# Masked copies of two units by one transfer per head, and the second unit's level products behind the turned attention

## The reference, cut to what matters

```python
xn = _ln(x, ln1_w, ln1_b); sx = _token_shift(xn, state[:, i1])
xxx = jnp.tanh((xn + sx * maa_x) @ maa_w1)...           # five mixes
w = jnp.exp(-jnp.exp(time_decay + jnp.tanh(x5[:, :, 1] @ decay_w1) @ decay_w2))
r, k, v = ...  ; g = jax.nn.silu(x5[:, :, 4] @ Wg.T)
def step(s, rkvw):
    a = k_t[:, :, :, None] * v_t[:, :, None, :]
    out = jnp.einsum('bhk,bhkd->bhd', r_t, u * a + s)
    return (a + w_t[:, :, :, None] * s, out)
att = group_norm(outs) * gn_w + gn_b
x = x + att * g @ Wo.T
xn2 = _ln(x, ln2_w, ln2_b); sx2 = _token_shift(xn2, state[:, i0])
rr = jax.nn.sigmoid((xn2 + sx2 * ffn_maa_r) @ ffn_Wr.T)
kk = jnp.square(jax.nn.relu((xn2 + sx2 * ffn_maa_k) @ ffn_Wk.T))
return x + rr * (kk @ ffn_Wv.T)
```

## Time and profile before

| | before |
|---|---|
| median of three runs | 1507.39 us |
| lowest, highest | 1506.85, 1512.62 us |
| the profiled execution | 1505.76 us |
| its span | 1504.0 us |
| TensorE matmuls busy | 1438.4 us, 96% |
| VectorE, ACT, POOL busy | 60%, 34%, 40% |
| rm copies | 1024 issues of 12 KB |
| s0 loads (S0, S1) | 32 issues of 256 KB |

### The profile page before, as it was taken

How to read it: one execution, slowest core, us unless ns; L and a number is a source line. 1 busy time by engine, 2 the same in 40 slices (tenths; PEclk the granted TensorE clock), 3 DMA queues, 4 the chain that set the end, 5 groups by cost and what they waited for, 6 DMA issues and landing times.

```text
span 1504.0 us, 51989 instructions
## 1 busy us (share of the span) xinstructions
PE 1438.4 (96%) x22954; PEld 1071.4 (71%) x22954; DVE 909.6 (60%) x1990; ACT 517.6 (34%) x911; POOL 599.2 (40%) x528
## 2 busy tenths in 40 slices
PE   8998999999999999999999999999999999999898
PEld 7776876767777676876767777676876767777464
DVE  3667557664675657657574775656657564665542
ACT  1323433323333333432433333333423433332332
POOL 3353516235362433616235362433616235262421
PEclk9999999999999999999999999999999999999899
DMA  8011101011110111101011010111102011010110
GB/s 311 7 49 44 41 26 57 17 41 54 32 59 7 41 54 38 55 22 61 18 41 54 29 56 13 41 55 38 55 10 73 17 41 54 14 55 15 57 31 28
DMA packets 56448, 68.11 MB, mean 45 GB/s; under 512 B 23264, under 2 KB 40032, under 8 KB 55200
## 3 DMA queue, kind: packets, MB, share of 16 engines
q1 hardware_dynamic: 56224, 64.79, 13.9%
HBM read 43.75 MB, written 8.39 MB: 35 GB/s over the span
## 4 chain that ended last, share of the span: by engine, by line
PE 81%; DVE 9%; SPq 4%; issue 2%; DMA 2%; ACT 1%; POOL 1%; DVEq 0%; ACTq 0%; POOLq 0%
PE pairs L1227 31%; PE pairs L1246 20%; PE at_ps L1155 4%; PE pairs L1238 4%; SPq L404 3%; PE at_ps L1148 3%; DVE x L781 3%; PE pairs L1254 3%; PE pairs L1270 2%; PE att_ps L1218 2%; PE pairs L1293 2%; PE pairs L1338 1%; PE pairs L1311 1%; PE pairs L1305 1%; DVE sx L881 1%
## 5 line engine op out<-in xcount | busy, mean ns | idle before, releaser
L1227 PE MATMUL pairs<-x,wts 128*128 128x256 f32 x1760 | 397.0, 380 | 1.1 <-DVE lag L805 0.4
L1227 PEld LDWEIGHTS pairs<-x,wts 128*128 128x128 f32 x1760 | 328.4, 190 | 51.2 <-issue 7.1
L978 ACT ACTIVATE at<-at_ps 128x512 f32<-128x512 f32 x128 | 76.4, 597 | 381.5 <-PE at_ps L1155 190.3
L551 POOL TENSOR_TENSOR x<-x,xnT 128x1024 f32<-128x1024 f32 (+1 forms) x79 | 158.5, 2006 | 63.4 <-DVE x L781 63.4
L781 DVE SCALAR_TENSOR_TENSOR x<-pairs,vecs,sx 128x256 f32<-128x256 f32 x316 | 129.0, 474 | 82.2 <-PE pairs L1270 72.1
L561 POOL TENSOR_TENSOR bonv<-bonv,lag 128x256 f32<-128x256 f32 x32 | 27.1, 847 | 226.8 <-DVE lag L801 226.8
L1227 PE MATMUL pairs<-yT,wts 128*128 128x256 f32 x512 | 113.8, 380 | 3.1 <-POOL yT L551 1.9
L1155 PE MATMUL at_ps<-rm,kc 128*16 128x128 f32 (+1 forms) x2048 | 111.8, 276 | 3.9 <-issue 3.9
L1246 PE MATMUL pairs<-wts,cen 128*128 128x512 f32 x240 | 107.2, 598 | 4.5 <-DVE x L781 4.5
L1246 PE MATMUL pairs<-wts,yT 128*128 128x512 f32 x240 | 107.1, 599 | 0.5 <-POOL yT L588 0.5
L1227 PEld LDWEIGHTS pairs<-yT,wts 128*128 128x128 f32 x512 | 95.9, 190 | 16.1 <-issue 2.0
(11 more groups left out here) (198 smaller groups left out, 2621.0 us busy)
## 6 DMA issues: line engine op xcount, KB each, us to landing
rm<-rst SPq DMA_DIRECT2D x1024, 12.0 KB, 1.8
xu<-in_x SPq DMA_DIRECT2D x16, 512.0 KB
wts<-in_wts SPq DMA_DIRECT2D x8, 1024.0 KB, 14.0
kvs<-in_s SPq DMA_DIRECT2D x32, 256.0 KB, 2.9
s<-in_s SPq DMA_DIRECT2D x32, 256.0 KB, 3.8
x<-in_x SPq DMA_DIRECT2D x15, 512.0 KB, 4.9
out<-sx SPq DMA_DIRECT2D x15, 512.0 KB, 3.0
prev<-in_prev SPq DMA_DIRECT2D x32, 4.0 KB, 3.6
```

Of the source, the lines that this page charges most:

```text
L551: gp.tensor_tensor(t, t, old, ALU.add).then_inc(x5_ready, 1)
L978: ac.activation(at[:, :, :], at_ps[:, :].rearrange("p (h t) -> p h t", h=HG), ACT.Copy)\
L1227: last = pe.matmul(ps[:, g // 2, TB * (g % 2):TB * (g % 2 + 1)], wts[:, m, k, g * P:(g + 1) * P], source[:, k, :], start=(k == 0), stop=(k ...
```

## The change

`rm` becomes one tile `rmp` with two halves, for an even and an odd unit, and its DMA semaphore is one in place of two. `mask` is called for even units alone; each of its eight DMAs takes one head's rows of two neighbouring units, 16 partitions by 2 by 192 floats. It waits until the level products of all units before n are through, so of the unit directly before it. M1, M3, M5 and M7 leave the three SP lists. In `PE_ORDER`, A1 moves from behind wv.1 to directly behind aT1, ahead of V0; no other order of TensorE changes, neither does any list of ACT, DVE and POOL, nor `BANK`.

```diff
-PE_ORDER = ["kt0", "V7", "hs_0", "kv0", "A0", "mixWV", "aT1", "V0", "wv.0", "wv.1", "A1", "vt_1", "V1", "hs_1", "A2", "V2",
+PE_ORDER = ["kt0", "V7", "hs_0", "kv0", "A0", "mixWV", "aT1", "A1", "V0", "wv.0", "wv.1", "vt_1", "V1", "hs_1", "A2", "V2",
...
-SP_ORDER = ["x", "S0", "M1", "F1", "M2", "M3", "out", "x2", "S1", "M4", "M5", "F0", "M6", "M7", "M0"]
+SP_ORDER = ["x", "S0", "F1", "M2", "out", "x2", "S1", "M4", "F0", "M6", "M0"]
...
-    0: ["M1", "x", "F1", "M2", "M3", "out", "x2", "S1", "M4", "M5", "F0", "M6", "M7", "M0"],
-    LAST: ["S0", "M1", "F1", "x2@0", "x2@1", "M2", "M3", "M4", "out", "x2", "S1", "M5", "M6", "M7"],
+    0: ["x", "F1", "M2", "out", "x2", "S1", "M4", "F0", "M6", "M0"],
+    LAST: ["S0", "F1", "x2@0", "x2@1", "M2", "M4", "out", "x2", "S1", "M6"],
...
-        rm = [sb(f"rm{p}", [P, HG, RMW]) for p in range(2)]
+        rmp = sb("rmp", [P, 2, HG, RMW])
+        rm = [rmp[:, p, :, :] for p in range(2)]
...
-                b, g, p = n // G, n % G, n % 2
-                if blk.past(UNITS, n - 1):
-                    sp.wait_ge(levels_done, blk.count(UNITS, n - 1))
+                b, g = n // G, n % G
+                if blk.past(UNITS, n):
+                    sp.wait_ge(levels_done, blk.count(UNITS, n))
                 sp.wait_ge(rchain, blk.count(2 * NR, NR * (b + 1)))
                 for h in range(HG):
-                    sp.dma_start(rm[p][S * h:S * (h + 1), h, :], rst[S * h:S * (h + 1), b, g, R16C:R64A])\
-                      .then_inc(rm_in[p], 16)
+                    sp.dma_start(rmp[S * h:S * (h + 1), :, h, :], rst[S * h:S * (h + 1), b, g:g + 2, R16C:R64A])\
+                      .then_inc(rm_in, 16)
...
-                pe.wait_ge(rm_in[p], at_.count(16 * HG * UNITS // 2, 16 * HG * (n // 2 + 1)))
+                pe.wait_ge(rm_in, at_.count(16 * HG * UNITS // 2, 16 * HG * (n // 2 + 1)))
```

More of the change, by code:

```diff
@@ L283, in build @@
         first_in = [sem(f"first_in{b}") for b in range(NB)]
-        rm_in = [sem(f"rm_in{p}") for p in range(2)]
+        rm_in = sem("rm_in")
         (att_ready, gsum_ready, gmean_ready, cen_ready, sq_ready, gvar_ready, gstd_ready, grs_ready, yn_ready,
```

## The result

| | before | after |
|---|---|---|
| median | 1507.57 us (4 runs) | 1534.03 us (4 runs) |
| lowest, highest | 1506.85, 1512.62 | 1531.84, 1534.56 |
| profiled execution, its span | 1505.76, 1504.0 | 1531.84, 1529.9 |

The changed kernel is slower: ratio 1.0165, interval 1.0141 to 1.019. The direction is as forecast, the size is not: 1518 was predicted, with a range of 1509 to 1527, so the loss is 26 us in place of 10.

What follows compares the result with a forecast made beforehand. TensorE, busy for 96% of the span, was taken as the bound. 8.1 + 1.6 + 1 - 1.5 + 1 = +10.2 on the profiled 1505.76 gave 1516.0, or 1518 against the median; range 1509 to 1527.

Steps and rivals of the forecast that it cites:

- The bound and the middle blocks: TensorE's instruction stream sets the end; in steps 2 to 14 wv.0 starts 0.62 us later per block, +8.1 us.
- What comes back behind wv: nothing: Steps 2 to 14: vt_1 still waits for VectorE's product of wv, so A1's old place becomes idle TensorE time.
- The faster rival: vt_1 finds its bank free, so A1's 1.23 us comes back behind wv: -8, about 1497; chance 0.06.
- The pauses: Unnamed TensorE stops between hs_0 and wv.0 grow with A1's 64 matmuls: +1.6 us, bounds -1 to +6.
- The copies in a middle block: Pairs land in time, 4 us to spare at M2 and 1.8 at M4; 0.6 us per issue taken.
- This is what A1's move buys: Middle blocks, M2: A1 ends early enough for the pair to be ready 4 us before A2 starts.
- The edges: Step 0 +1 us (0 to +3), step 1 -1.5 (-3.4 to +0.5), last step +1 (0 to +3).
- M6 and M0 have the dense products of wo and g, or kk and rr, in between: Middle blocks: these products separate odd unit from next even one, so M4, with 1.8 us to spare, is narrowest.
- The working of 6.5 us per set: Eight issues of 0.589 us plus 1.8 landing: each even unit needs 6.5 us after the odd unit's end.
- The last step: A2 waits until 1417.3, A5's wait of 1.07 goes, M6 is ready at 1442.5: +1 us (0 to +3).
- the order: A1 ahead of V0 in TensorE's stream, 13 blocks of steps 2 to 14: 0.62 us each, +8.1 us.

Runs made afterwards that it cites:

- the first experiment: The changed kernel with vt_1 turning the values into the other pair of banks (BANK entry 0 in place of 1): 1541.64 us, ratio 1.0214.
- the old edges: The changed kernel with single copies and the earlier TensorE and SyncE orders in blocks and steps 0, 1 and the last: 1522.59 us, ratio 1.0077.

## Why the prediction was wrong

Step by step, by its own parts:

- **The bound and the middle blocks: right.** TensorE's stream sets the end. A1 and V0 as neighbours take 1.78 us, the number taken from the earlier trace rows; the rule of the Trainium skill in "TensorEngine Tiling (Array Packing)", Key Properties, that a change of tiling mode drains the array, stays in agreement with that row, though no run separates a drain from other costs of a change. 13 x 1.78 = 23.1 us stand now where V0 and the wait of wv.0 took 15.8 (the sum of the 13 stretches from V0 to wv.0 in before): +7.4, against +8.1 predicted. "What comes back behind wv: nothing" is exact: 127.99 and 128.02 us, with 1.32 us of waiting in all 13 blocks.
- **The faster rival: wrong in two ways.** vt_1 didn't find its bank free: it waited 1.32 us in all 13 blocks, as the forecast had it. And freeing that bank (the first experiment) doesn't give A1's time back: VectorE's 6 us behind wv hold v.0, a second bound that the prediction did not look for.
- **The pauses: mis-sized.** Priced at +1.6 with a bound of +6, they are +5.8 by the same cut: the 13 stretches from A1 to wv.0 sum to 30.4 us, 7.3 more than 13 x 1.78, less 1.5 that went between hs_0 and aT1. Of the causes named, F1's place gave no time back (its experiment); A1's 64 matmuls next to the others stay: between the halves of wv they left the stretch ahead of wv.0 as it was. What TensorE waits for in a pause the list of waits doesn't say, but the trace points to its own instructions. The page counts the transfers that bring instructions, the same in before and after (packets, MB, share of 16 engines):

```profile
q8 instruction: 181, 2.97, 0.8%
```

That is one transfer for some 254 of TensorE's 2 x 22954 matmuls and weight loads. In steps 2 to 14 TensorE has 10 idle times over 0.2 us without a releaser in before, 6.4 us, and 18 in after, 10.6 us, and all 28 end 2.2 to 2.9 us behind the start of such a transfer, a place that takes up 9% of the time. A run of small matmuls would use up a transfer soonest. No run varied this, so it is a strong hint and not shown.

- **The copies in a middle block: right.** No A in steps 2 to 14 waits for a copy; the four waits are at 84.63, 128.56, 1441.93 and 1467.46, in step 0 and in the last step, and to these come two under the name issue, 1.4 us behind the end of their copies' issue: A0 at 144.91 and A4 of the last step at 1453.76. An issue takes 0.593 us. "This is what A1's move buys" is shown by the copies alone, 1599 us.
- **The edges: the step that failed.** "M6 and M0 have the dense products of wo and g, or kk and rr, in between" is true of a middle block and was carried to steps 0 and 1, for which the sum then had only A2's wait. In step 0 there is no block i-1 yet, so no wo, kk or rr. A5 ends at 122.1, and A6 starts at 128.56, 6.4 us later, after 2.16 us of waiting. The working of 6.5 us per set was right and would have given this, had it been applied to each even unit of each edge step. M0 of block 1 then waits for A7 in turn and goes out 8.8 us later; A0 waits 3.35, mixWV and VectorE's chain come late behind it, and hs_1 waits 4.51. Steps 0 and 1 were priced at -0.5 together and took +10.7: 4.3 up to A3 of step 0 (A2's wait, priced at +1, with the low clock behind it), 2.2 for A6 (at nothing), 4.15 in step 1 (at -1.5). This is 11 of the 16 us by which the forecast was short, and the old edges give it back, 10.4 of 10.7.
- **The last step: mis-sized**, +1.9 for +1; A4's wait of 3.39 us there was priced at nothing.

The size adds up: +10.2 predicted, +11.2 more for steps 0 and 1, +4.2 for the pauses, -0.7 for the order, +0.9 at the last step, -0.4 at the start and +0.7 elsewhere in the middle blocks make 26.1 by these rounded terms; the spans differ by 25.9.

The Trainium skill, "DMA: Bandwidth & Descriptors", Rules for kernel authors, says to coalesce small transfers. The price of an issue agrees with it: twice the bytes cost 593 in place of 589 ns. But the issues were hidden before, and the pair has to wait for one unit more: alone it costs 89 us.

No kernel measured here beats the one before; the nearest, with V0 behind wv and the old edges, has the ratio 1.0029 (1.0008 to 1.005).

## What to carry to other kernels

When a buffer is coupled to a neighbour's, work out the time from the last reader to the next one for every step of the pipeline, and do it again for the first and last steps, where the stages that gave cover are missing. Work placed ahead of an engine's long stage is paid in full, while work behind it is free up to what the reader of that stage needs; look for the second bound there before counting a freed bank as a gain. Where an early start depends on a queue, follow the queue back past the load in front of it.

## What the runs showed of the hardware that was not expected

- A DMA of 24 KB is issued in 593 ns and lands 1.9 us later, one of 12 KB in 589 ns and 1.8 us.
- Two waits of 0.46 and 1.53 us with 0.47 us of matmuls between them were followed by a granted clock of 0.58 over 4 us in one block and by 1.00 in another; it fell in 7 of 13 blocks. A wait of 2.92 was followed by 0.54 over 3 us (0.50 is the lower level, 1.2 of 2.4 GHz). A single wait of 1.32 us ahead of vt_1, in 13 blocks, left the time behind it unchanged.
- The pauses of TensorE grew by 5.8 us in 13 blocks when 64 small matmuls joined a run of small ones, and the stretch ahead of wv.0 kept its time when they stood between long ones. All 28 idle times over 0.2 us without a releaser in steps 2 to 14 of before and after end 2.2 to 2.9 us behind the start of an instruction transfer.
- A row of VectorE of 0.42 us took 2.17 when it started 0.1 us behind an operation of POOL of 2.02 us, in 12 of 13 blocks.
